# Large cross-attention on one Trainium2 core: keys turned from their natural layout a batch ahead, a new order of the engines' steps, and the odd heads' last four additions on GpSimd

## What is computed

```python
q_big = einsum('bshk,hkq->bshq', (hidden_q @ Wq.T).reshape(B, S, H, K), w_kc_q)
q_big = rope(q_big)
kv_r = rope(kv_c)                       # 1601 x 64 per batch
scores = einsum('bhsr,bhlr->bhsl', q_big @ W_qr, kv_r @ W_kr)
attn = softmax(scores)
ctx_c = einsum('bhsl,bld->bhsd', attn, kv_r)
out = ((ctx_c @ w_kc_kv.T) over heads) @ Wo.T
```

## Time and profile before

| what | us |
|---|---|
| median of 3 runs | 3505.46 |
| lowest, highest | 3505.07, 3515.96 |
| profiled execution | 3504.15 |
| its core span | 3501.6 |
| large attention, first value product of batch 0 to last of batch 31 | 766.4 to 2627.2 |
| one pair of batches in the steady state | 119.5 |

### The profile page before, as it was taken

How to read it: one execution, slowest core, us unless ns; L and a number is a source line. 1 busy time by engine, 2 the same in 40 slices (tenths; PEclk the granted TensorE clock), 3 DMA queues, 4 the chain that set the end, 5 groups by cost and what they waited for, 6 DMA issues and landing times. The chain is left out here.

```text
span 3501.6 us, 51568 instructions
## 1 busy us (share of the span) xinstructions
PE 2942.5 (84%) x17592; PEld 1773.8 (51%) x17592; DVE 2084.2 (60%) x3249; ACT 1277.2 (36%) x2482; POOL 900.8 (26%) x784
## 2 busy tenths in 40 slices
PE   6767734579988988898898889888996889999999
PEld 3544412445544544454455445444543457777776
DVE  3445567357686777677776877686775643333332
ACT  3433312123344343434334433444343333333332
POOL 0001000134354444344434544453440000000000
PEclk9888856679999999999999999999999899999999
DMA  1000030000000000000000000000003000000000
GB/s 39 0 17 0 0 117 0 22 19 10 19 9 19 9 19 9 19 9 19 9 11 17 19 9 9 19 9 19 10 0 145 0 0 0 0 0 0 0 0 25
DMA packets 15045, 57.83 MB, mean 17 GB/s; under 512 B 2512, under 2 KB 7248, under 8 KB 13584
## 3 DMA queue, kind: packets, MB, share of 16 engines
q1 hardware_dynamic: 13392, 53.57, 5.5%
q10 hardware_dynamic: 1600, 3.56, 0.3%
HBM read 55.03 MB, written 2.10 MB: 16 GB/s over the span
## 5 line engine op out<-in xcount | busy, mean ns | idle before, releaser
L917 ACT ACTIVATE cx_prob<-cx_st 128x512 f32<-128x512 f32 (+1 forms) x832 | 477.4, 596 | 742.8 <-PE cx_st L774 680.7
L645 POOL TENSOR_TENSOR cx_acc<-cx_acc,cx_prob 128x512 f32<-128x512 f32 (+1 forms) x352 | 493.8, 1403 | 751.5 <-ACT cx_prob L917 747.4
L1023 DVE TENSOR_REDUCE cx_mhalf<-cx_mx 128x1 f32<-128x804 f32 x512 | 491.2, 983 | 86.5 <-PE cx_mx L747 83.7
L785 PE MATMUL cx_av<-cx_prob,cx_kv 128*64 128x512 f32 (+1 forms) x1664 | 462.2, 635 | 0.0
L773 PE MATMUL cx_st<-cx_q,cx_k 128*128 128x512 f32 (+1 forms) x832 | 372.5, 448 | 84.5 <-ACT cx_prob L917 60.5
L1506 PE MATMUL moe_gu<-moe_wgu,moe_xnT 128*128 128x352 f32 x1280 | 399.0, 463 | 0.0
L1044 DVE TENSOR_TENSOR cx_acc<-cx_acc,cx_prob 128x512 f32<-128x512 f32 (+1 forms) x352 | 371.3, 1055 | 21.7 <-ACT cx_prob L917 19.9
L747 PE MATMUL cx_mx<-cx_k,cx_q 128*128 128x402 f32 x1024 | 309.3, 388 | 53.2 <-DVE cx_mhalf L1023 47.3
L1641 DVE SCALAR_TENSOR_TENSOR moe_hid<-moe_silu,moe_coef,moe_gu 128x176 f32<-128x176 f32 x320 | 127.1, 397 | 351.6 <-ACT moe_silu L1569 349.4
L774 PE MATMUL cx_st<-cx_q,cx_k 128*128 128x512 f32 (+1 forms) x832 | 332.8, 400 | 0.0
L747 PEld LDWEIGHTS cx_mx<-cx_k,cx_q 128*128 128x128 f32 x1024 | 173.4, 195 | 264.0 <-DVE cx_mhalf L1023 216.8
(11 more groups left out here) (214 smaller groups left out, 3945.0 us busy)
## 6 DMA issues: line engine op xcount, KB each, us to landing
cx_ctx<-in_cx_ctxT SPq DMA_DIRECT2D x32, 402.0 KB, 4.3
cx_ctxr<-in_cx_ctxrT SPq DMA_DIRECT2D x32, 402.0 KB, 5.5
moe_wgu<-in_moe_wgu SPq DMA_DIRECT2D x5, 1408.0 KB, 15.3
moe_wd<-in_moe_wd SPq DMA_DIRECT2D x4, 896.0 KB, 25.0
x_all<-in_x SPq DMA_DIRECT2D x1, 2048.0 KB, 5.3
cx_wq<-in_cx_wq SPq DMA_DIRECT2D x1, 2048.0 KB, 12.0
cx_woT<-in_cx_woT SPq DMA_DIRECT2D x1, 2048.0 KB, 29.5
out_x<-x_all SPq DMA_DIRECT2D x1, 2048.0 KB, 7.5
```

What stands on the lines that cost most here:

```text
L645: pool.tensor_tensor(acc[0][rows, :], sofar, prob[slot(kt)][rows, 0, :], ALU.add)\
L785: last = pe.matmul(av[DCX * p:DCX * p + DCX, :], kv[e][0:nk(kt), kt, :], prob[slot(kt)][0:nk(kt), p, :], start=(kt == 0), stop=(kt == NKT ...
L917: act.activation(prob[slot(kt)][rows, p, :], st[p][rows, :], ACT.Exp).then_inc(s_exp, 1)
L1023: dve.tensor_reduce(mhalf[:, i // 2, i % 2:i % 2 + 1], mx[i % 2][:, :, 0:KQ], AX.XY, ALU.max)\
```

## The change

Keys and values:
- The context comes key-major: 128 partitions x 13 tiles x 64 features, twice. GpSimd rotates it in two operations of 832 columns, VectorE adds it in one. This `kr` is already the value operand, which ScalarE copies into `kv`.
- ScalarE writes the high part and VectorE the low part side by side into `khl`. TensorE turns each tile as one 128 x 128 transpose (high and low features together), in four groups of up to four tiles; ScalarE copies each group into `kp`.
- The max-score pieces read `kp`. SP moves `kp` into `k1`, and its upper half into `k2`, with two DMAs within SBUF per batch; the score products wait for them.
- The turning is for two batches ahead, the rotation on GpSimd for three.

Order of the steps:
- Queries are made in the even batch, tiles 7 to 11, and copied and split in the odd batch, tiles 0 to 2.
- Pieces lie in tiles 1 to 6 of the even batch and 3 to 9 of the odd one.
- Output at tile 5, both rows of maxima at tile 11 in `mx`, two tiles behind the negated maxima of tile 9.
- In tiles 9 to 12 GpSimd makes the odd heads' additions too.

```diff
-    OUT_AT = 4
-    TURN_AT = 6
-    ROWS_AT = NKT - 3
-    SUM_AT = (8, 9, 11, 12)
     HEADS_AT = 2
+    OUT_AT = 5
+    SUM_AT = 4
+    KH_AT = 6
+    KL_AT = 7
+    TURN_AT = 7
+    QUERIES_AT = 7
+    NORM_AT = 10
+    NEGATE_AT = 9
+    ROWS_AT = 11
+    HANDED_AT = 9
     def pieces(e, kt, third):
-        start, end = 3 * (5 if e else 3), 3 * ROWS_AT
+        start, end = (9, 3 * NEGATE_AT + 3) if e else (4, 3 * QUERIES_AT)
...
+            def move(n, e):
+                sp.wait_ge(s_kp, KROUNDS * (n + 1))
+                if not isinstance(n, int) or n >= 2:
+                    sp.wait_ge(s_st, (n - 1) * 2 * NKT)
+                sp.dma_start(k1[e][:, :].bitcast(F32), kp[e][:, 0:SKP].bitcast(F32)).then_inc(s_kd[e], 16)
+                sp.dma_start(k2[e][0:DCX, :].bitcast(F32), kp[e][0:DCX, 0:SKP].bitcast(F32)).then_inc(s_kd[e], 16)
...
@@ SyncE @@
+            def batch(n, t, e, more, next, far):
+                if next:
+                    move(n + 1, 1 - e)
+                if far:
+                    sp.wait_ge(s_kr, n + 3)
+                    fetch(n + 3)
...
@@ GpSimd @@
+            def add_odd(n, kt):
+                rows = slice(0, nk(kt))
+                pool.wait_ge(s_exp, n * 2 * NKT + 2 * kt + 2)
+                pool.wait_ge(s_acc[1], n * NSUM + kt - 1)
+                pool.tensor_tensor(acc[1][rows, :], acc[1][rows, :], prob[slot(kt)][rows, 1, :], ALU.add)\
+                    .then_inc(s_acc[1], 1)
...
                 for kt in range(1, NKT):
                     add(n, kt)
-                    if more and kt % 2 == 1 and 3 <= kt < 3 + 2 * NKC:
-                        rotate(n + 2, kt // 2 - 1)
-                    if more and e == 0 and kt == ROWS_AT:
-                        root(t + 1)
+                    if kt >= HANDED_AT:
+                        add_odd(n, kt)
+                    if kt == NORM_AT and far and e == 1:
+                        root(t + 2)
+                    if kt == NORM_AT and far:
+                        rotate(n + 3)
...
@@ TensorE @@
+            def turn_keys(n, r):
+                if r == 0:
+                    pe.wait_ge(s_kl, n + 1)
+                else:
+                    pe.wait_ge(s_kp, KROUNDS * n + r)
+                for kt in range(4 * r, min(4 * r + 4, NKT)):
+                    last = pe.transpose(misc[:, kt % 4 * P:(kt % 4 + 1) * P], khl[:, kt, :, :], ident[:, :])
                 last.then_inc(s_kt, 1)
...
                 for kt in range(NKT):
-                    if kt == 0 and more and e == 1:
-                        turn_x(t + 1)
...
-                        if more and e == 1 and third < 2 and kt <= CP // 2:
-                            queries(t + 1, 2 * kt + third)
+                        if more and e == 0 and third < 2 and 0 <= kt - QUERIES_AT <= CP // 2:
+                            queries(t + 1, 2 * (kt - QUERIES_AT) + third)
                         if next:
                             for i in pieces(e, kt, third):
                                 max_scores(t + e, n + 1, 1 - e, i)
+                            if kt == ROWS_AT and third == 1:
+                                max_rows(n + 1, 0)
+                                max_rows(n + 1, 1)
+                    if kt == QUERIES_AT - 1 and more and e == 0:
+                        turn_x(t + 1)
...
@@ ScalarE @@
                 for kt in range(NKT):
                     exps(n, kt)
...
-                    if kt == 0 and next:
-                        keep_keys(n + 1, 1 - e, k1, s_k1)
+                    if kt in (0, 1) and more and e == 1:
+                        keep_queries(t + 1, kt)
                     if kt == 1 and next:
-                        keep_keys(n + 1, 1 - e, k2, s_k2)
...
+                        keep_kv(n + 1, 1 - e)
+                    if kt == KH_AT and more:
+                        keep_kh(n + 2)
+                    if kt == QUERIES_AT and more and e == 0:
+                        keep_x(t + 1)
+                    if 0 <= kt - TURN_AT - 1 < KROUNDS and more:
+                        keep_turned(n + 2, t + 1, e, kt - TURN_AT - 1)
+                    if kt == ROWS_AT and next:
+                        keep_rows(n + 1, 1 - e, 0)
+                        keep_rows(n + 1, 1 - e, 1)
...
@@ VectorE @@
                     for third in range(3):
-                        if third == 1 and kt:
+                        if third == 1 and 0 < kt < HANDED_AT:
                             add(n, kt)
-                        if third < 2 and more and e == 1 and kt < CP // 2:
-                            rotate(t + 1, 2 * kt + third)
+                        if third < 2 and more and e == 0 and 0 <= kt - QUERIES_AT < CP // 2:
+                            rotate(t + 1, 2 * (kt - QUERIES_AT) + third)
...
-                    if kt == 1 and next:
-                        keep_kl(n + 1, 1 - e)
+                    if kt in (1, 2) and more and e == 1:
+                        split(t + 1, kt - 1)
...
+                    if kt == SUM_AT and more:
+                        sum_keys(n + 2)
+                    if kt == KL_AT and more:
+                        keep_kl(n + 2)
...
+                    if next and kt == NEGATE_AT:
+                        negate_max(n + 1, base + 2 * e)
+                    if kt == NORM_AT and far and e == 1:
+                        gather(t + 2, base + 4)
+                    if kt == NORM_AT + 2 and far and e == 1:
+                        normalise(t + 2)
```

More of the change, by code:

```diff
@@ L403 @@
 KQ = SKP // 4
-KC = 402
-NKC = SKP // KC
 NKT = -(-SK // P)
+SKT = NKT * P
+KROUNDS = 4
 NSUM = NKT - 1
@@ L494, in context_attention @@
     tab = sb("cx_tab", [P, 2, 3, S])
[L495 to L499, removed]
+    kcos = sb("cx_kcos", [P, NKT, DCX])
+    ksin = sb("cx_ksin", [P, NKT, DCX])
+    ctx = sb("cx_ctx", [P, NKT, DCX])
+    ctxr = sb("cx_ctxr", [P, NKT, DCX])
+    kr = sb("cx_kr", [P, NKT, DCX])
+    khl = sb("cx_khl", [P, NKT, 2, DCX])
+    kp = [sb(f"cx_kp{i}", [P, SKT], F32R) for i in range(2)]
     k1 = [sb(f"cx_k1{i}", [P, SKP], F32R) for i in range(2)]
@@ L611, in fetch, with before, rotate @@
             def fetch(n):
[L612 to L619, removed]
+                sp.dma_start(ctx[:, :, :], a["cx_ctxN"][bass.ds(n, 1), :, :, :]).then_inc(s_ctx, 16)
+                sp.dma_start(ctxr[:, :, :], a["cx_ctxrN"][bass.ds(n, 1), :, :, :]).then_inc(s_ctx, 16)
+            def move(n, e):
[4 more added lines that the diff above has]
+                sp.dma_start(k2[e][0:DCX, :].bitcast(F32), kp[e][0:DCX, 0:SKP].bitcast(F32)).then_inc(s_kd[e], 16)
+            def before():
+                fetch(0)
+                sp.wait_ge(s_kr, 1)
+                fetch(1)
+                sp.wait_ge(s_set, 6)
+                move(0, 0)
+                sp.wait_ge(s_kr, 2)
+                fetch(2)
+            def batch(n, t, e, more, next, far):
[4 more added lines that the diff above has]
+                    fetch(n + 3)
+            batches(sp, before, batch)
         @block.gpsimd
         def _(pool):
[L623 to L628, removed]
+            def rotate(n):
+                pool.wait_ge(s_ctx, 32 * n + 32)
+                pool.tensor_tensor(ctx[:, :, :], ctx[:, :, :], kcos[:, :, :], ALU.mult)
+                pool.tensor_tensor(ctxr[:, :, :], ctxr[:, :, :], ksin[:, :, :], ALU.mult).then_inc(s_rope, 1)
             def root(t):
@@ L656, in before, with batch @@
                 root(0)
[L657 to L661, removed]
+                rotate(0)
+                rotate(1)
+                root(1)
+                rotate(2)
+            def batch(n, t, e, more, next, far):
                 for kt in range(1, NKT):
                     add(n, kt)
-                    if more and kt % 2 == 1 and 3 <= kt < 3 + 2 * NKC:
-                        rotate(n + 2, kt // 2 - 1)
-                    if more and e == 0 and kt == ROWS_AT:
-                        root(t + 1)
+                    if kt >= HANDED_AT:
[4 more added lines that the diff above has]
+                        rotate(n + 3)
             batches(pool, before, batch)
@@ L672, in _ @@
         def _(pe):
[L673 to L680, removed]
-                        pe.matmul(o, keys, ident[0:DCX, 0:DCX], start=True, stop=True)
-                    else:
-                        last = pe.transpose(o, keys, ident[0:DCX, 0:DCX])
+            def turn_keys(n, r):
[5 more added lines that the diff above has]
+                    last = pe.transpose(misc[:, kt % 4 * P:(kt % 4 + 1) * P], khl[:, kt, :, :], ident[:, :])
                 last.then_inc(s_kt, 1)
@@ L808, in before @@
                 pe.wait_ge(s_one, 1)
-                turn_keys(0, 0)
-                turn_keys(0, 1)
+                for r in range(KROUNDS):
+                    turn_keys(0, r)
                 turn_x(0)
@@ L815, in before, with batch @@
                     max_scores(0, 0, 0, i)
+                for r in range(KROUNDS):
+                    turn_keys(1, r)
                 max_rows(0, 0)
```

(23 more changed lines are left out.)

147 lines of the change are left out of this document (64 added, 83 removed).

## The result

| | before | after |
|---|---|---|
| median of 4 runs each, us | 3509.53 | 3547.65 |
| profiled execution | 3504.15 | 3547.55 |
| core span | 3501.6 | 3545.8 |
| ratio, 95% interval | | 1.0114 [1.0083, 1.0146] |
| first value product of batch 0 to last of batch 31 | 1861.2 | 1904.8 |

The account below looks back on a forecast made before the run. TensorE was taken as nearly the bound, busy 106.2 of a 119.5 us pair. A pair of 121.6 against 119.3 gave +35; first and last batches and preparation brought +37: median 3542 us, range 3450 to 3580.

Parts of the forecast that it names:

- The pair: Even plus odd batch of the large attention: 74.6 and 47.0 us, together 121.6, against a mean of 119.3 before.
- Opening of the even batch: First tile of the even batch: TensorE waits 1.4 us for denominators, as GpSimd ends its odd-batch work late.
- VectorE's chain in the even batch: Reductions, additions, inversions, scaling and key sum run in order, with idle during the output; last reduction ends at 32.2 us.
- Key turn behind the low part: Even batch, after tile 7: the turn waits for the low part behind VectorE's second rotation, TensorE idle 1.1 us.
- ScalarE's opening of the odd batch: Odd batch start: ScalarE's copies delay tile 2's exponentials, so the third value product comes at 7.7 us, not 5.2.
- Odd chain to the twelfth reduction: Odd batch: VectorE's work from tile 2's addition at 7.2 us through reductions, inversions, scaling and key sum ends at 29.5.
- Key turns: TensorE's thirteen key transposes in four groups: 1.9 us a batch, bounds 1.8 and 2.6, or +0.5 a batch.
- Key move at nothing: SP's moves of turned keys within SBUF cost 0; bounds 0 and 16 us a batch, first read some 45 us later.
- The rest: Outside the steady pairs: preparation 2 us longer, batch 30 in batch 0's place 1 shorter, batch 31 1 longer.
- faster: Rival for the large attention: half of some 12 us of waits never reaches TensorE; pair 115.6, total 3450; chance 0.32.
- Slower by the clock: Rival: two more clock falls at TensorE's idle gaps cost 1.2 us each, +2.4 a pair, total 3578; chance 0.12.
- No difference: Rival: waits removed equal waits made, pair within 0.7 us of 119.3, total 3495 to 3516; chance 0.13.

Follow-up runs that it names:

- the repeated run: The changed kernel run again with nothing changed: 3555.59 us, ratio 1.0163, mean pair 122.23 us.
- the doubled move: Changed kernel, with SP moving the turned keys a second time into a tensor nothing reads, and their readers waiting for it: 3560.78 us, mean pair 122.23.
- the later key turn alone: Changed kernel with keys turned from tile 8 instead of 7: 3495.93 us, ratio 0.9994, mean pair 118.8 us.
- with the inversions: Changed kernel with keys turned from tile 8, odd-batch inversions at the ends of tiles 0 and 1, scaling behind the second split: 3453.32 us, ratio 0.9863.
- the fastest version: Changed kernel: keys turned from tile 8, kv copy behind tile 3, odd-batch inversions earlier, scaling behind second split, GpSimd additions from tile 5: 3400.44 us, ratio 0.9712.

## Why the prediction was right

The forecast, slower by 37 us at 3542, came out at 3547.65, slower by 38. The mechanism was right: VectorE's chain among the pieces, the key turn behind the low part, ScalarE's opening and GpSimd's end are the waits that the trace shows. That the total came within 1 us is in part luck. The terms of the large attention, as measured, add up to +50, and the repeated run was slower by 54. In the profiled execution an earlier start took 10 of it back. Point by point, against the steady pair (122.9) and the mean (122.2):

- **The pair, 121.6**: even batch 74.6, measured 75.6; odd 47.0, measured 47.3. The odd batch has two errors that cancel: a clean one lasts 45.9, 1.1 under the sum, and a fall of the clock, which the sum leaves out, puts 1.4 on top. Another error helps the mean: batch 0, which follows no other batch, lasts 66.0, and the sum took it as 74.6. The steady pair alone was forecast 1.3 too short.
- **Opening of the even batch**: TensorE waiting 1.4 for GpSimd, measured 1.52. The reason given was partly wrong. The step counted eight additions, the root and both rotations as one block of 15 us; without four of the additions the wait was 1.43. What places the end is the root's wait for VectorE's variance, with the rotations behind it.
- **VectorE's chain in the even batch, end at 32.2** (its own terms add up to 32.4): measured 33.6 (last reduction from 1644.29 to 1645.27). Of the difference, 1.0 is the key sum, taken at 1.0 and found at 2.0, since a GpSimd addition had just started (GpSimd, then VectorE, in the changed kernel):

```profile
1633.88 1.30 POOL L682 TENSOR_TENSOR cx_acc<-cx_acc,cx_prob 128x512 f32<-128x512 f32 x1 [4.41 <-ACT cx_prob L956]
...
1634.04 2.01 DVE L1017 TENSOR_TENSOR cx_kr<-cx_ctx,cx_ctxr 128x832 f32<-128x832 f32 x1
```

  The idle of 2.9 during the output was 2.60; the wait of the turned x, 0.85, was 1.58.
- **Key turn behind the low part, even batch 1.1**: 1.04. Tiles 8 to 10 at 8.58 each: 8.52. Tile 11 6.4, tile 12 2.6, next 2.1: 6.27, 2.67, 2.13.
- **ScalarE's opening of the odd batch, third value product at 7.7**: 7.6, with the wait of 1.81 ahead of it.
- **Odd chain to the twelfth reduction 29.5**: 28.8. **Low part 1.1** from there to the key turn: 1.0. The term of the sum held, but in the count of waits it stood as 1.1 too, and TensorE waited 2.02. It stands at the turn as soon as its piece is issued, one reduction earlier.
- **Key turns, 1.9 a batch, bounds 1.8 and 2.6**: 1.3 from start to next score in a clean batch (0.41 for a group of four, 0.09 for the last), under the lower bound. The 1.7 in the odd batch's sum was 0.4 too much.
- **Other prices**: 832 columns on ScalarE 0.87, measured 0.88; on VectorE 1.0, measured 1.015; rotations at most 2.1, measured 1.96 and 2.00. All lines through two rows held where no operation of GpSimd was beside them.
- **Key move at nothing**: shown by the doubled move.
- **The rest**: preparation +2, measured +4.1 (75.2 against 71.1 from GpSimd's first rotation to the first value product); batch 30 in batch 0's place -1, measured -0.7; after the last value product +1, measured +3.4 (14.7 against 11.3 to the last update of x). With 15 x 2.9 the terms give +50. The profiled execution shows +43.4, because its preparation began 10 us earlier than in the one before, and the stages behind the large attention took 3 us longer, both in stages that the change leaves alone.

Of the rivals, *faster* stood on the waits of the kernel before getting a tile of room. Those for maxima, rows and heads went; that for exponentials stayed, 3.2 after 3.9. Its 115.6 a pair was there to be had: the later key turn alone gives 118.8, with the inversions 115.5. *Slower by the clock* did not happen: granted at half for 48 us between 830 and 2500, 55 before. One fall costs 1.4 here, where the rival took 1.2. *No difference* is excluded by the interval.

The marks set for it: odd 46 to 48 and even 73 to 76 held, and so did the idle ahead of the even batch's first key turn and GpSimd releasing the denominators. "VectorE over 95% busy from odd tile 3 to 8" failed: 19.3 of 22.2 us, 87%. VectorE's idle 2.7 us behind the key turn were left out of that mark; without them it is 99%.

What the prediction undervalued is how cheap the cure was. It named the key turn as 1.1 + 1.1 us among seven waits. It was 3.1, and one constant.

## What to carry to other kernels

- When the order is written by hand, a step whose input the same tile's end produces on another in-order engine stops both in turn: the reader stands, then the producer has nothing to do. One tile between the low part and its turn was worth 3.5 us of 122. Two steps of one engine (split, scaling) in the wrong order ate two thirds of a gain in the same way (0.8 instead of 2.3 us).
- Relieving a busy engine counts only where it sets the pace. Four additions a batch taken off it in tiles 9 to 12 brought 0.0 us; eight, from tile 5, brought 1.5 alone and 2.3 once the other waits were gone. In clean batches these two are 1.7 and 2.1, so most of their difference is falls of the clock.
- Compare by a mean over the repeated stage when single per cents matter, and look at repetitions without a fall of the clock beside it: shares that seemed not to add did add there. The stages ahead of it moved the whole time by up to 18 us here.

## What the runs showed of the hardware

- VectorE's operations on two SBUF operands that started behind one of GpSimd's were stretched from 0.67 to 2.17, from 1.02 to 1.83, and from 1.0 to 2.0 us. They ended 0.6, 0.9 and 0.9 us behind the end of GpSimd's, which is nearly the whole of what they take alone. The Trainium skill (SBUF — State Buffer, "SBUF: two separate sides") says that whichever of the two starts first holds the shared ports for its whole instruction and the other blocks. All three agree. Placing GpSimd's two-microsecond operations beside them cost 5.5 us a pair, the falls of the clock that came with it included. I had expected a loss of tenths.
- Two DMAs within SBUF, 0.8 and 0.4 MB, landed 3.9 and 5.1 us after issue, and 0.8 MB more beside them left the pair unchanged to 0.01 us.
- One idle gap of TensorE of about 2 us costs more than its length when the clock falls at it: about 1.4 us more in an odd batch (45.9 without a fall, 47.3 with one, 48.5 with two, in the changed kernel). There 13 of the 14 falls between 830 and 2500 began within 0.5 us of the end of one of the odd batch's two gaps, 1.8 and 2.0 us long. So 13 of some thirty such gaps had a fall. Behind the even batches' gaps of up to 1.7 us there was none. In the fastest version, with no gap over 1.7 us in the pair shown, the clock was full but for 3.4 us of 1670.
